# When the gathers of an embedding-interaction kernel are let go, and where PE's transposes and dense pieces stand in its order

## The reference, cut to what matters

```python
e = jnp.stack([tbl_f[ids[:, f]] for f in range(32)], axis=1)      # 1024 x 32 x 64
p, q = e[:, iu, :], e[:, ju, :]                                    # 496 pairs
z = jnp.einsum('bpe,fpe,bpf->bp', p, kernel, q)
h = jnp.concatenate([z, dense_ctx], axis=1)                        # 1024 x 512
h = jnp.maximum(h @ W_top1 + b_top1, 0.0)
h = jnp.maximum(h @ W_top2 + b_top2, 0.0)
y = h @ W_top3
```

## Time and profile before

| | us |
|---|---|
| median of 3 runs | 492.27 |
| lowest and highest | 491.04 and 494.61 |
| the profiled execution, its own time | 495.03 |
| its span, first to last instruction | 493.0 |
| granted TensorE clock in it | 0.997 of full speed |

### The profile page before, as it was taken

The page is one execution under the profiler, slowest core; times in us unless marked ns, Lnnn a source line. Parts: engine busy times, 40 slices in busy tenths (PEclk is TensorE's granted clock), DMA queues, the critical chain, the costliest instruction groups (busy, mean ns, idle before and its releaser), DMA issues.

```text
span 493.0 us, 12100 instructions
## 1 busy us (share of the span) xinstructions
PE 406.5 (82%) x4144; PEld 277.7 (56%) x4144; DVE 347.8 (71%) x438; ACT 333.8 (68%) x2552; POOL 241.7 (49%) x260
## 2 busy tenths in 40 slices
PE   0620069898889888999989899999999999999997
PEld 0400046565556555676657566667666667666775
DVE  0000079888888787778878888788888888899830
ACT  1210064436995899588877797869687978999842
POOL 5777445556566655555555565556655663000000
PEclk9999999899999999999999999999999999999999
DMA  8731141113211111011110111111111110000000
GB/s 279 253 93 26 19 145 21 21 22 112 61 22 20 23 23 23 19 23 21 21 23 21 21 23 21 23 23 20 23 21 22 22 23 15 2 2 1 2 1 0
DMA packets 12756, 19.16 MB, mean 39 GB/s; under 512 B 6037, under 2 KB 6297, under 8 KB 12569
## 3 DMA queue, kind: packets, MB, share of 16 engines
q0 software_dynamic: 8192, 8.40, 9.2%
q1 hardware_dynamic: 2592, 8.29, 4.9%
q10 hardware_dynamic: 1912, 1.71, 1.2%
HBM read 18.39 MB, written 0.00 MB: 37 GB/s over the span
## 4 chain that ended last, share of the span: by engine, by line
PE 72%; DVE 10%; another core or an unknown queue 8%; issue 8%; ACT 2%; ACTq 0%; DVEq 0%
PE t_ps L538 25%; PE z_ps L608 13%; PE t_ps L568 12%; PE t_ps L555 9%; PE prep_ps L623 5%; DVE prod L446 5%; PE prep_ps L579 3%; DVE prod_a L466 3%; PE prep_ps L670 2%; PE t_ps L623 2%; DVE prod_a L485 1%; DVE zb L472 1%; PE t_ps L670 1%; ACT prod_a L388 1%
## 5 line engine op out<-in xcount | busy, mean ns | idle before, releaser
L388 ACT ACTIVATE prod_a<-prod_a 128x64 f32<-128x64 f32 x1232 | 295.1, 243 | 53.2 <-DVE prod_a L501 29.0
L342 POOL DMA_INDIRECT raw<-tbl,ids_sb x256 | 241.5, 943 | 171.6 <-PE t_ps L538 51.4
L388 ACT ACTIVATION_READ_ACCUMULATOR prod_a<-prod_a 128x1 f32 x1232 | 233.1, 189 | 0.7 <-issue 0.5
L446 DVE TENSOR_TENSOR prod<-t_ps,xt 128x1024 f32<-128x1024 f32 x128 | 155.5, 1220 | 74.5 <-remote 35.9
L538 PEld LDWEIGHTS t_ps<-xt,k_sb 64*128 64x128 f32 x2048 | 135.8, 190 | 50.8 <-issue 30.6
L538 PE MATMUL t_ps<-xt,k_sb 64*128 64x128 f32 x2048 | 151.7, 283 | 13.7 <-DVE prod L446 6.2
L466 DVE TENSOR_TENSOR prod_a<-t_ps,raw 128x1024 f32<-128x1024 f32 x64 | 77.9, 1217 | 17.0 <-PE t_ps L568 15.4
L485 DVE TENSOR_TENSOR prod_a<-t_ps,raw 128x768 f32<-128x768 f32 (+2 forms) x96 | 62.8, 682 | 33.2 <-PE t_ps L555 24.2
L568 PE MATMUL t_ps<-k_sb,xt 64*128 64x512 f32 x256 | 73.3, 646 | 8.0 <-issue 4.8
L555 PE MATMUL t_ps<-k_sb,xt 64*128 64x384 f32 (+5 forms) x448 | 69.1, 406 | 6.1 <-issue 4.3
L364 ACT ACTIVATE xt<-prep_ps 128x512 f32<-128x512 f32 (+2 forms) x47 | 20.9, 444 | 73.9 <-remote 40.8
(11 more groups left out here) (28 smaller groups left out, 77.3 us busy)
## 6 DMA issues: line engine op xcount, KB each, us to landing
raw<-tbl,ids_sb POOLq DMA_INDIRECT x256
k_sb<-kmat SPq DMA_DIRECT2D x4, 768.0 KB
k_sb<-kmat SPq DMA_DIRECT2D x4, 512.0 KB
k_sb<-kmat SPq DMA_DIRECT2D x4, 448.0 KB, 4.6
k_sb<-kmat SPq DMA_DIRECT2D x4, 256.0 KB
w_sb<-w ACTq DMA_DIRECT2D x1, 1024.0 KB
w_sb<-w ACTq DMA_DIRECT2D x1, 512.0 KB
ids_sb<-ids SPq DMA_DIRECT2D x1, 128.0 KB, 2.5
```

The costliest lines, as they stand in the source:

```text
L342: nc.gpsimd.indirect_dma_start(raw[:, n % RING, begin:begin + EMBED], None, tables[2 * k + f], bass.IndirectOffsetOnAxis(ap=ids_sb[:, t, 2 ...
L388: last = nc.scalar.activation(product, product, ACT.Copy, accum_out=zb[:, unit[1], at:at + 1])
L446: nc.vector.tensor_tensor(prod[:, own].rearrange("p n (m b) -> p (n m) b", b=P), t_ps[:, slot].rearrange("p n (m b) -> p (n m) b", b=P), x ...
```

## The change

The change moves work in time and alters no instruction but the waits in front of gathers.

1. Gathers of slices 1 to 7 wait for 8 units more: field f of slice t waits for unit (t - 1) * 32 + f, where it was t * 32 - 40 + f.
2. In slice 0 the fields from 16 on are paced too. Fields 16 and 17 wait for unit 2, fields 18 and 19 for unit 3, and so on to fields 30 and 31 for unit 9.
3. The fills of slices 4 to 7 come one unit later. Their rank is behind that of sums of the same place, so they then stand directly behind a round's sums. In slice 3 the four fills are moved by -4, -1, 0 and 1 units.
4. Turns and pieces come one unit later (17 and 25 instead of 16 and 24). Eight units of slices 4 to 6 now go: C, piece, F, B, F, C, sums, fill, F, B, F. Directly behind sums stand, newly, 14 fills (the last two of slice 4 and the twelve of slices 5 to 7); one of slice 3 that stood so doesn't any more.
5. At the very end the order was: last F unit, piece 5 of the third quarter, the last turn, the last but one sums, piece 6. It becomes: last F unit, the last turn, the last but one sums, piece 5, piece 6.

```diff
-GATHER_AHEAD = 40
...
-TILE_UNITS = NU
+def gather_after(t, field):
+    return (t - 1) * NU + field if t else (field - 12) // 2 if field >= 16 else 0
...
-    return [(packs, begin + (g - 2) * 8 - 4) for g, packs in enumerate(groups)]
-GROUPS_AT = {3: (-6, -3, 4, 10), 4: (-19, -12, -4, 4)}
+    return [(packs, begin + (g - 1) * 8 - 11) for g, packs in enumerate(groups)]
+GROUPS_AT = {3: (-10, -4, 4, 11), 4: (-18, -11, -3, 5)}
 PAIRS_AT = {1: (-5, -2, 1, 4, 8, 13, 17), 2: (-6, -2, 1, 4, 8, 12, 20)}
...
-TURN_LAG, PIECE_LAG, PIECE_STEP = 16, 24, 8
+TURN_LAG, PIECE_LAG, PIECE_STEP = 17, 25, 8
...
-                    pace = t * TILE_UNITS - GATHER_AHEAD + 2 * k + f
-                    if t and pace > 0:
-                        pool.wait_ge(t_done, pace)
+                    if gather_after(t, 2 * k + f) > 0:
+                        pool.wait_ge(t_done, gather_after(t, 2 * k + f))
```

## The result

| | before | after |
|---|---|---|
| median of 4 runs each, side by side | 492.49 | 485.65 |
| lowest and highest | 491.04 and 494.61 | 484.71 and 487.7 |
| the profiled execution | 495.03 | 486.05 |
| its span | 493.0 | 484.0 |
| granted TensorE clock | 0.997 | 0.965 |

The ratio is 0.9864, with an interval of 0.9815 to 0.9912: faster by 6.8 us, where 23 were forecast. The two profiled executions differ by 9.0 us, since that of the kernel before lies 2.5 us above its median and that of the changed kernel 0.4. In some sessions the long waits of the start are there and the kernel before takes 492 to 503 us, in others none are there and it takes 422, so each ratio here is made against the kernel before in the same session.

The account below looks back on a forecast made before the run. PE sets the pace (busy 406 of 493 us), and in the start gathers hold it. Pacing -24, one more gather group +1.3, fills -2.0 and end +1.4 sum to -23.3 us: median 492.3 to 469, range 455 to 494.

Parts of the forecast that it names:

- What bounds the start: Start of slice 0: POOL's back-to-back gathers hold back PE's completions or their counting, 34.3 us; chance of the forecast 0.75.
- the first rival: Start: the hold has another cause and ends when it ends, gathers or none; 493 us (489 to 495), chance 0.13.
- the two signs of being wrong: In the profile after: DVE's long wait stands at 60 us still, or the hold returns in pieces behind each gather group.
- Pacing slice 0: Slice 0: gathers from 16 on wait for units, so POOL pauses and frees PE; -24 us, the middle of 14.2 and 37.
- the closed end: Slice 0's lower bound: gathers 16 to 40 hold PE nearly all the while, unit 9 through by 59.2; 14.2 us won.
- the open end: Slice 0's upper bound: POOL's catching up doesn't hold PE at all; 34.3 us won, up to 37.
- One more group with gathers at the end, +1.3: Slices 1 to 7: the last gather waits for unit 223, not 215, so eight more units run with gathers; +1.3 us.
- Fills behind sums, -2.0: Late slices: fills directly behind sums lose one of two PE gaps, 13 x 0.15 = -2.0 us, bounds 0 and -4.
- The end, +1.4: Program end: the turn fills piece 5's old place, piece 5 follows the sums, piece 6 waits for ACT; +1.4 us (0 to 2).
- The cover of the fills: Slice 0: paced gathers still land before PE's fills need them; were it gone, each fill would wait 1 to 3 us.
- Slower by catching up, 512 us: Start: POOL's catching up holds PE as the unpaced run did, if the release comes after 44.6; 512 us, chance 0.10.
- Only the order counts, the hold is a feature of one execution: Start: the median holds none of the hold; given little, with the first rival's time, within their shared chance of 0.13.

## Why the prediction was right or wrong

*What bounds the start: right.* Gathers hold the other engines. The measured 485.65 us lies between the forecast's 455 to 481 and the first rival's 489 to 495, in neither. The number of free gathers set the end of the hold in three kernels: 33 free, DVE goes on at 52.4; 41 free, at 63.7; 65 free, at 90.4, after a single unit at 75.8. Of what I had named as signs, DVE took the first F unit before 35 us, POOL was busy nearly without pause from 26 to 59.8, F units take 2.33 us beside gathers; but one wait of over 10 us is left. Of the two signs of being wrong, the first came true: DVE's long wait still ended at 61.17. The rule of the Trainium skill, page "SBUF — State Buffer", section "SBUF: two separate sides", that transfers and compute don't slow each other, went with the first rival and its 493 us. The plain transfers agree with it (DVE busy for 33.04 of 37 us beside 36 of them), and so does everything in the sessions without the hold. In the sessions with it the other engines do stand beside indirect ones. That is no proof against the rule, since as many bytes in as many packets on POOL's queue held nothing in the plain form; it shows that the rule isn't enough to say that gathers cost the engines nothing.

*Pacing slice 0: the mechanism right, the size wrong.* The step that failed is "I see nothing that is nearer to one of them and take the middle, 24 us". The bounds were 14.2 (the run of catching up holds PE nearly all the while) and 34.3 or 37 (it doesn't hold PE). It came to 12.2 us, just beyond the closed end and 11.8 less than the term. The row for it stood in the earlier trace rows: 17 gathers at 1.25 us each with PE, DVE and ACT at nothing. The catching up was forecast as the same 1.25 us each, so it was nearly the same condition, and the nearest row was that one, though units 5 to 9 came through beside the first of the run. What spoke for the open end, the first 20 us, was thin: PE had hardly any work there to be held. I had also tied that end to the wrong event. I argued that unit 9 must be through before POOL's last permission; it was through much sooner (DVE took it at 42.52, not 73.42), POOL had its last permission by 45.1, and then 12 more gathers, up to number 41 at 58.85, waited for no unit. The hold lasted as long as that run. The unit behind, the tenth, reached DVE at 61.17 instead of 74.99: 13.8 us, the closed end after all, since what sets it is the end of POOL's run (59.2 forecast, 59.8 measured).

*The clock of PE: not costed.* Between units 10 and 11 the lead over the kernel before falls from 13.8 to 12.6 us, and this isn't the clock: unit 11's matmuls (57.02) ended at 59.1, and DVE waited for them until 64.69 by the same unnamed wait, 1.11 us. Between units 13 and 14 it falls from 12.7 to 10.7 us, and there DVE waits 2.38 us for PE. In this stretch the F unit at 65.10 takes 2.08 us and the sums behind it 3.24, both at a granted clock of 0.50, where at 1.00 they take 1.16 and 1.93. By the end of slice 0 1.6 us of it have come back; I can't split these. The 1.00 of the earlier trace rows says nothing of PE's speed: that trace has no record of the clock before 67.6 us, and a stretch without one is shown as 1.00. Its first F unit behind the release took as long as those at 0.50. First the kernel before, then the changed one:

```profile
64.46 2.08 PE L538 MATMUL t_ps<-xt,k_sb 64*128 64x128 f32 x16
```
```profile
67.11 3.24 PE L613 MATMUL z_ps<-prod,sel_sb 128*32 128x256 f32 x32
```

*What the term really was.* The smaller number ahead gives the gain without the pacing of slice 0: with 32 ahead and no pacing slice 0 is done at 103.0, with both at 102.1. This is across two sessions, so the 0.9 us between them are no safe price of the pacing. What pacing would give with 40 ahead was not run. I had costed the smaller number at nothing for the start ("the term above") and given it all to the pacing.

*One more group with gathers at the end, +1.3:* it came as +2.4 in slice 6. With 32 ahead and the old order slice 6 takes 52.5 us where the kernel before took 50.5; across two sessions, then, some 2.0 of it belong to the gathers. By the run without late gathers the price is 26 us over 128 units, 1.6 for eight; 1.3 was a little low.

*Fills behind sums, -2.0: not seen where the hold is, and right where it isn't.* With it, slices 4 and 5 are 0.7 and 0.8 us longer, and the order alone has the ratio 0.9998. With the same waits in slices 1 to 7, slices 3 to 6 take 213.5 and 216.2 us with the new order and 211.0 and 214.7 with the old one, in four different sessions, so the order may even cost something there. Without the hold they take 186.2 and 188.4: -2.2 us. Small gaps on PE count only where PE is the last. That beside the gathers it is the delay of PE's completions that counts, and not the length of its queue, is my reading; no run tried it apart.

*The end, +1.4:* +0.8 to 0.9, in sessions of both kinds. The turn and the sums took the place that piece 5 had, as forecast; the size was too large by half a microsecond.

*The cover of the fills* was sufficient: no wait of PE for gathered rows stands in the chain behind the start.

*Slower by catching up, 512 us:* it needed a release later than 44.6. The release came at 27.1, since POOL was out of permitted gathers. What was right in that rival is that the second run holds too, though not as fully (PE busy for 6.57 of 21 us, where the first left it nothing). *Only the order counts, the hold is a feature of one execution:* wrong, but the hold is in fact no property of the kernel alone. Had I been in a session without it, 421 against 422 would have been the result.

*Still open:* why the hold is there in some sessions and not in others. The chip numbered 9 showed 503 us in one session and 422 in two; chips 4 and 0 showed 503 and 494. I found nothing in the profiles that tells the two kinds apart but the waits, and none of the runs was made to tell what differs.

## What to carry to other kernels

An unpaced run of indirect DMAs on POOL can stop every other engine, and pacing only the first run moves the stop to the run in which POOL catches up: here the hold ended some microseconds behind POOL's run wherever that run ended, so look for the run that takes the place of the one removed, and for the number of gathers let go in all. Between two bounds far apart, ask of each which row shows the very condition that the new schedule makes, and go to that end; the middle is the value for which no row speaks. Measure a change that lives from such waits in more than one session before believing its size: here it is 1.4 to 2.2% in one kind and 0.2% in the other.

## What the runs showed of the hardware

- Indirect DMAs issued by POOL 1.25 us apart kept PE's, DVE's and ACT's work from going on for up to 45 us in one piece. The hold ended 3 to 8 us after the start of the last gather of POOL's run: 45.9, 56.1, 56.4 and 87.2 us, the first of the others on again at 52.4, 63.7, 63.3 and 90.4 (there after a single unit at 75.8). At 1.55 us apart most of it was gone (DVE busy for 16.38 of 21 us).
- The same bytes by plain DMAs from POOL (in as many packets) or SP, with near or scattered rows, held nothing; gathers of rows 0 to 127 in order held as much as random ones.
- In sessions with this effect, gathers that come one for each unit cost 1.6 us for eight units; in sessions without it nothing (slices 3 to 6 took 188.4 us there with the old order and all gathers, as in the kernel without late gathers).
- The granted clock of the changed kernel was 0.50 from 35.7 to 69.8 us, a stretch in which PE was busy for 6.57 of 21 us at first, and 1.00 behind it, where the units came densely; an F unit took 2.08 us at 0.50 and 1.16 at 1.00. A granted clock of 1.00 shown ahead of a trace's first record of it says nothing: the F unit at 64.46 of the kernel before took 2.08 us there.
